# Weights, x and the result laid out by features: an adaptive-layer block on one core without its TensorE turns outside attention and the gates

## The reference

```python
c = einsum('bti,oi->bto', x, W1) + b1 + 2.0 * (x @ lora_As[id1]) @ lora_Bs[id1]        # (b, t, 1024)
# attention inside a sequence, rotary, causal: 32 query heads, 8 key/value heads of 128
a = softmax(mask(rope(c @ wq) . rope(c @ wk) * 128**-0.5)) . (c @ wv)
x1 = x + a @ wo
# two more layers behind each other, each a base weight and gated low-rank parts
d = x1 @ W2.T + 2.0 * sum_e gate_e * (x1 @ A2_e.T) @ B2_e.T               # 8 experts, top 2, language bias
y = x1 + d @ Wf.T + bf + 0.5 * sum_e combine_e * (d @ Af.T) @ Bf_e.T      # 16 experts, top 2 of softmax(d @ Rf.T)
```

## Time and profile before

| | us |
|---|---|
| median of 3 runs | 2720.73 |
| lowest, highest | 2719.8, 2721.68 |
| the profiled execution | 2716.21 |
| its span in the profile | 2714.4 |
| TensorE busy (PE) | 2662.1 |
| VectorE, ScalarE, GpSimd busy | 1341.2, 842.3, 1060.9 |

### The profile page before, as it was taken

One profiled execution on the slowest core, in us unless ns is written; L12 is line 12 of the kernel. 1 busy time (PEld: TensorE's weight loads), 2 busy tenths in 40 slices (PEclk: granted clock), 3 DMA queues, 4 the chain that ended last, 5 costly groups with the idle time before them and its releaser, 6 DMA issues.

```text
span 2714.4 us, 36233 instructions
## 1 busy us (share of the span) xinstructions
PE 2662.1 (98%) x13880; PEld 2135.4 (79%) x13880; DVE 1341.2 (49%) x2035; ACT 842.3 (31%) x2041; POOL 1060.9 (39%) x686
## 2 busy tenths in 40 slices
PE   8989999999999999999999999999999999999999
PEld 7867777777776788887877777777777678888877
DVE  3134677777777111124533577777777511113442
ACT  2132344444444211221212334444444422121110
POOL 0035666666665334520304553344343453341120
PEclk9999999999999999999999999999999999999999
DMA  6953233333335333111534323333332551311322
GB/s 213 235 188 117 90 127 113 111 121 125 125 117 202 132 109 116 47 39 54 145 122 112 123 95 113 113 113 113 113 112 87 182 181 53 116 47 40 96 81 65
DMA packets 335917, 312.45 MB, mean 115 GB/s; under 512 B 71674, under 2 KB 282746, under 8 KB 335746
## 3 DMA queue, kind: packets, MB, share of 16 engines
q1 hardware_dynamic: 274146, 254.55, 30.1%
q10 hardware_dynamic: 61600, 55.58, 6.2%
HBM read 220.75 MB, written 89.33 MB: 114 GB/s over the span
## 4 chain that ended last, share of the span: by engine, by line
PE 88%; POOL 5%; DMA 2%; DVE 1%; issue 1%; SPq 1%; ACT 1%; POOLq 0%; ACTq 0%; DVEq 0%
PE prod L704 27%; PE prod L705 26%; PE prod L706 26%; PE turned L951 3%; PE turned L905 2%; POOL o_lo L1567 1%; PE turned L698 1%; PE prod L1131 1%; POOL w_lo L1484 1%; PE turned L920 1%; POOL s_lo L1520 1%; DMA raw<-in_wo 1%; PE prod L815 1%; POOL x_sum L1502 1%; PE turned L935 0%
## 5 line engine op out<-in xcount | busy, mean ns | idle before, releaser
L1484 POOL TENSOR_TENSOR w_lo<-raw,w_hi 128x1024 fp32r<-128x1024 f32 x96 | 238.9, 2490 | 811.5 <-ACT w_hi L1191 811.5
L704 PE MATMUL prod<-o_hi,w_hi 128*128 128x512 f32 x1024 | 403.1, 394 | 14.2 <-POOL o_lo L1567 10.3
L705 PE MATMUL prod<-o_lo,w_hi 128*128 128x512 f32 x1024 | 399.3, 390 | 0.0
L706 PE MATMUL prod<-o_hi,w_lo 128*128 128x512 f32 x1024 | 399.1, 390 | 0.0
L1860 DVE TENSOR_TENSOR x<-prod,x 128x512 f32<-128x512 f32 x128 | 88.5, 691 | 563.9 <-PE prod L706 563.9
L1520 POOL TENSOR_TENSOR s_lo<-w_sum,s_hi 128x512 fp32r<-128x512 f32 x192 | 249.7, 1307 | 295.1 <-ACT s_hi L1251 295.1
L1191 ACT CAST w_hi<-raw 128x1024 fp32r<-128x1024 f32 x130 | 136.2, 1048 | 609.5 <-PE prod L706 432.1
L704 PE MATMUL prod<-t_hi,s_hi 128*128 128x512 f32 x768 | 311.7, 406 | 8.0 <-POOL s_lo L1520 8.0
L705 PE MATMUL prod<-t_lo,s_hi 128*128 128x512 f32 x768 | 301.3, 392 | 0.0
L706 PE MATMUL prod<-t_hi,s_lo 128*128 128x512 f32 x768 | 300.6, 391 | 0.0
L1520 POOL TENSOR_TENSOR s_lo<-raw_pair,s_hi 128x512 fp32r<-128x512 f32 x144 | 198.2, 1383 | 149.2 <-ACT s_hi L1251 145.3
(11 more groups left out here) (167 smaller groups left out, 4824.7 us busy)
## 6 DMA issues: line engine op xcount, KB each, us to landing
o_scratch<-o_out ACTq DMA_DIRECT2D x64, 512.0 KB, 3.2
raw<-in_wo SPq DMA_DIRECT2D x64, 512.0 KB, 3.8
o_raw<-o_scratch SPq DMA_DIRECT2D x64, 512.0 KB, 7.1
raw<-t_scratch SPq DMA_DIRECT2D x50, 512.0 KB, 3.7
raw_pair<-in_wq SPq DMA_DIRECT2D x48, 512.0 KB, 3.9
w_sums_scratch<-w_sum SPq DMA_DIRECT2D x96, 256.0 KB, 4.4
w_sum<-w_sums_scratch SPq DMA_DIRECT2D x96, 256.0 KB, 4.5
t_scratch<-x ACTq DMA_DIRECT2D x17, 512.0 KB, 5.2
```

What stands on the lines that cost most here:

```text
L704: pe.matmul(dst, wh, xh, start=start, stop=False)
L705: pe.matmul(dst, wh, xl, start=False, stop=False)
L706: return pe.matmul(dst, wl, xh, start=False, stop=stop)
L1484: pool.tensor_tensor(WL[i % 2][:], RAW[i % 2][:], WH[i % 2][:].bitcast(F32), ALU.subtract).then_inc(w_lo, 1)
```

## The change

The host lays x, Wf, Af with Rf, Wr2, W1, A2, Bf and B2 out with the input feature on the partition axis, and takes the result by features. The kernel loses all turns but those of attention and of the gates.

- Wf is loaded in 16 pieces of 256 KB, first the eight of t = 0, then W2's second block, then the eight of t = 1. ScalarE casts from SBUF piece by piece, VectorE splits, and the first product of the fold waits chunk by chunk. The turns, copies, stores and loads of `tw` go; each tile is read from the input where it is needed. B2 comes in one transfer instead of eight.
- The first tile of W1 is loaded in the fold's last iteration, cast after the product of i = 7, and split by GpSimd. `fold_buf` exchanges the two `raw` buffers for this. Tile 1 is loaded there too, but is cast after the fold.
- x of t = 0 is loaded, cast and split inside the fold (hf 0) or in the output stage (hf 1), in place in the room of `xt_lo`. x of t = 1 is loaded by 8 transfers of 256 KB that stand on SyncE's queue behind `b_rows` and ahead of W1's tile 2; ScalarE casts its first four chunks after tile 2 and the rest after tile 3; VectorE splits four of them ahead of `h_mask(0)` and four behind it.
- GpSimd's sum, its store and its DRAM copy go; X1 is loaded from x.
- `out_t` is stored straight after VectorE's addition, and its buffer is written again when the store has landed; `turn_out` and `out_s` go.

```diff
...
-        XR = [sb(f"x_raw{i}", [P, D], offset=o * KB) for i, o in enumerate((0, 4, 8, 12, 36, 40, 44, 32))]
...
+        XTR = [sb(f"xt_raw{t}", [P, KC * NT], offset=o * KB) for t, o in enumerate((48, 128))]
...
+            sp.dma_start(ES[:], arf).then_inc(small_in, 16)
+
+            def load_wf(t, k):
+                a = k * D + t * NT
+                sp.dma_start(X1[:, a:a + NT], Wf[:, a:a + NT]).then_inc(wf_in[t][k], 16)
 
             def load_w2(i):
-                sp.dma_start(view(RAW[i % 2][:], KC), W2.rearrange("(k p) n -> p k n", p=P)[:, :, i * P:(i + 1) * P]
-                             ).then_inc(fold_in[i % 2], 16)
-
-            for b in range(KC // 2):
-                load_wf(b)
+                sp.dma_start(view(RAW[fold_buf(i)][:], KC),
+                             W2.rearrange("(k p) n -> p k n", p=P)[:, :, i * P:(i + 1) * P]
+                             ).then_inc(fold_in[fold_buf(i)], 16)
+
             load_w2(0)
-            for b in range(KC // 2, KC):
-                load_wf(b)
+            for k in range(KC):
+                load_wf(0, k)
             load_w2(1)
+            for k in range(KC):
+                load_wf(1, k)
...
-            def load_tw(n):
-
-                if n < 4:
-                    sp.wait_ge(fold_turned, n + 2)
-                else:
-                    sp.wait_ge(tw_turned, n - 4 + 1)
-                if n < TW_A2:
-                    src, dst = W1[n * P:(n + 1) * P, :], TW_IN[n % 4]
-                elif n == TW_A2:
-                    src, dst = A2, TW_IN[n % 4]
-                else:
-                    o = n - TW_B
-                    src = Bf[:, o * P:(o + 1) * P, :].rearrange("e p r -> p e r")
-                    dst = TW_IN[n % 4].rearrange("p (e r) -> p e r", e=EF)
-                sp.dma_start(dst, src).then_inc(tw_in[n % 4], 16)
-
             def adapter(hf, n):
                 return sp.value_load(ID1[0:1, hf * (BATCH // HALVES) + n:hf * (BATCH // HALVES) + n + 1],
                                      min_val=0, max_val=SLOTS - 1)
@@ -461,21 +435,22 @@
                     sp.dma_start(view(AWS[hf][:, t * D:(t + 1) * D], KC, n8 * RANK1, (n8 + 1) * RANK1),
                                  A1[bass.ds(m * D, D), :].rearrange("(k p) r -> p k r", p=P)).then_inc(a_in, 16)
 
-            def load_x(hf, b):
-                if hf == 0 and b >= 4:
-
-                    r = (b - 3) % 4
-                    sp.wait_ge(m_out[r], 16 * (KC // 4 + (r == 0)))
-                sp.dma_start(XR[b][:], x[hf * TOK + b * P:hf * TOK + (b + 1) * P, :]).then_inc(x_in[b], 16)
-
-            for n in range(4):
-                load_tw(n)
-            for i in range(2, KC + 1):
-                if 4 <= i < 8:
-                    load_x(0, i - 4)
-                if i >= 5:
-
-                    sp.wait_ge(const_in, 16 * 5)
+            def load_x(hf, t):
+                for k in range(KC):
+                    a = k * NT
+                    sp.dma_start(XTR[t][:, a:a + NT], x[hf * KC + k][:, t * NT:(t + 1) * NT]
+                                 ).then_inc(x_in[t][k], 16)
...
+                    load_tile(0, i - KC - 1, tw[TW_W + W1_ORDER[i - KC - 1][0]])
...
-            def store_xt(hf, b):
-                sp.wait_ge(x_sum, hf * TB + b + 1)
-                sp.dma_start(xt_d.rearrange("k p n -> p k n")[:, :, b * P:(b + 1) * P], view(XS[b % 2][:], KC)
-                             ).then_inc(xt_out[b % 2], 16)
...
-                    sp.dma_start(X1[:, j * TOK:(j + 1) * TOK], xt_d[j]).then_inc(x1_in[j], 16)
+                    sp.dma_start(X1[:, j * TOK:(j + 1) * TOK], x[hf * KC + j]).then_inc(x1_in[j], 16)
...
+                if hf:
+                    sp.wait_ge(prod, q_base)
+                load_x(hf, 1)
...
-            def turn_wf(b):
-                pe.wait_ge(wf_in[b], 16)
-                if b >= 1:
-                    pe.wait_ge(fold_split, b)
-                turn_block((b + 1) % 2, X1[:, b * D:(b + 1) * D], P, fold_turned)
...
-                        if i == 0 and t == 0 and k % 2 == 1:
-                            turn_wf(KC // 2 + k // 2)
-                        if i >= 1 and k == KC // 2:
-                            turn_tw(2 * (i - 1) + t)
-                        if i == KC and t == 1 and k == KC - 2:
-                            turn_tw(TW_N - 1)
-
-                    main(3 * i + 1 + t, i % 2, flat(XH, t), parts(XLP, t), chunk=chunk).then_inc(fold_prod, 1)
-
-            pe.wait_ge(tw_copied, TW_N)
+                        if i == 0:
+                            pe.wait_ge(fold_split, t * KC + k + 1)
+
+                    main(3 * i + 1 + t, fold_buf(i), flat(XH, t), parts(XLP, t), chunk=chunk).then_inc(fold_prod, 1)
+
...
-                def first_chunk(k):
-                    if k % 2 == 1:
-                        turn_x(hf, 4 + k // 2)
-
-                pe.wait_ge(xt_lo, hf * TB + 4)
+                pe.wait_ge(xt_lo, xt_no(hf, 0, KC - 1))
                 hold(pe)
-                c_main(0, chunk=first_chunk)
+                c_main(0)
...
-                def turn_out(q):
-                    for t in range(TT):
-                        pe.wait_ge(taken, q_base + (q - 2 + t + 1 + 4))
-                        for b in range(BPT):
-                            mm = pe.transpose(PJ[(q + t) % 4][:, b * P:(b + 1) * P],
-                                              OT[t][:, b * P:(b + 1) * P], ident)
-                        mm.then_inc(prod, 1)
-
...
+            def wf_hi(t, k):
+                act.wait_ge(wf_in[t][k], 16)
+                a = k * D + t * NT
+                act.copy(XH[:, a:a + NT], X1[:, a:a + NT]).then_inc(fold_hi, 1)
...
+            def x_hi(hf, t, k):
+                act.wait_ge(x_in[t][k], 16 * (hf + 1))
+                xs = slice(k * NT, (k + 1) * NT)
+                act.copy(XTH[t][:, xs], XTR[t][:, xs]).then_inc(xt_hi, 1)
...
+                if i == KC:
+
+                    act.wait_ge(fold_prod, 3 * KC)
+                    tile_hi(0, 0)
...
+                    for k in range(4 * n, 4 * n + 4):
+                        x_hi(hf, 1, k)
...
-                    pool.tensor_tensor(view(XS[b % 2][:], KC), view(XTH[t][:].bitcast(F32), KC, c, c + P),
-                                       view(XTL[t][:].bitcast(F32), KC, c, c + P), ALU.add).then_inc(x_sum, 1)
...
+            def wf_lo(t, k):
+                dve.wait_ge(fold_hi, 2 + t * (KC + 1) + k)
+                a = k * D + t * NT
+                dve.tensor_tensor(chunk_of(XLP, k, t), X1[:, a:a + NT], XH[:, a:a + NT].bitcast(F32), ALU.subtract
+                                  ).then_inc(fold_split, 1)
...
+            def x_lo(hf, t, k):
+                dve.wait_ge(xt_hi, xt_no(hf, t, k))
+                xs = slice(k * NT, (k + 1) * NT)
+                dve.tensor_tensor(XTL[t][:, xs], XTR[t][:, xs], XTH[t][:, xs].bitcast(F32), ALU.subtract
+                                  ).then_inc(xt_lo, 1)
...
+                for k in range(KC // 2):
+                    x_lo(hf, 1, k)
                 h_mask(0)
+                for k in range(KC // 2, KC):
+                    x_lo(hf, 1, k)
...
-                def take_out(s):
-                    q = Q_O + 4 * s + 2
-                    for t in range(TT):
-                        is_prod(q + t)
-                        dve.wait_ge(out_done[t], (hf * KC + s) * 16 + 16)
-                        dve.tensor_copy(OS[t][:], PJ[(q + t) % 4][:]).then_inc(taken, 1)
...
-        "x": np.asarray(x).reshape(BATCH * SEQ, D),
+        "x": np.asarray(x).reshape(HALVES, TOK, KC, P).transpose(0, 2, 3, 1).reshape(HALVES * KC, P, TOK),
...
```

More of the change, by code:

```diff
@@ L192, in build @@
         OT = [sb(f"out_t{t}", [P, NT], offset=(184 + 2 * t) * KB) for t in range(TT)]
-        OS = [sb(f"out_s{t}", [P, NT], offset=(188 + 2 * t) * KB) for t in range(TT)]
         BC = [sb(f"c2_cols{i}", [P, P], offset=(196 + i) * KB) for i in range(2)]
@@ L329, in hold @@
             eng.sem_inc(held[eng.engine], 1)
-        def tw_round(n):
-            return 16 * (n // 4 + 1)
-        def tw_all_stored(eng, last=TW_N - 1):
-            for n in range(last - 3, last + 1):
-                eng.wait_ge(tw_stored[n % 4], tw_round(n))
         def m_all_out(eng):
@@ L693, in _ @@
             pe.wait_ge(ident_in, 16)
-            def turn_block(par, raw, rows, done):
-                for c in range(KC):
-                    mm = pe.transpose(TP[par][:, c * P:c * P + rows], raw[0:rows, c * P:(c + 1) * P],
-                                      ident[0:rows, 0:rows])
-                mm.then_inc(done, 1)
             def three(dst, wh, wl, xh, xl, start, stop):
```

273 lines of the change are left out of this document (88 added, 185 removed).

## The result

The changed kernel takes **2677.03 us** (median of 4 runs, 2675.31 to 2679.09) against 2720.94 us before (4 runs). The ratio is 0.9836, with a 95% interval of 0.9823 to 0.9849. The gain is 43.9 us by the medians; I had forecast 50.3 and a time of 2670.4, with a range of 2661 to 2681. The profiled execution took 2678.42 us with a span of 2676.6. That of before (2716.21) was 4.7 us under its median, this one is 1.4 over its own, so the two traces differ by only 37.8 us in span. I compare places inside the traces first, then the medians.

A forecast was written before the change was run, and what follows sets the result against it. TensorE, busy 2662.1 of 2714.4 us, was taken to set the time, so work off its list counts in full. The terms sum to -50.3 us, span 2664.1, forecast 2670.4 us by the median, range 2661 to 2681 (80%).

The forecast's parts named there:

- A: Start, up to the fold's i = 1: without turns the data decide, 23.5 instead of 35.72 us, -12.2 us.
- B: Rest of the fold: two turns go per i, the pitch falls from 14.51 to 12.69 us, -16.9 us.
- C: Fold's end to `c_main(2)`: turns go but `c_lora(0)` newly waits for `h_masked`, 35.15 to 26.1 us, -9.0 us.
- D: Output stage: `turn_out` goes, a column takes 12.67 instead of 13.57 us; -9.0 us in half 0, -6.3 in half 1.
- E: Change of halves, to half 1's `c_main(2)`: a new wait as in half 0, 25.96 to 30.5 us, +4.5 us.
- F: Last instructions: the final store can start when `out_t` is done, not `out_s`, -1.4 us.
- The price of a turn: In the fold: six matmuls with one turn take 2.26 us, without it 1.36, so a turn costs TensorE 0.90 us.
- Small transfers pay alone: Loads of Wf and x: each 256 KB transfer takes 4.5 us, one after another; 77 us slower, 2798; chance 2%.
- The fold stays paced by its loads: Fold, i = 5 to 8: SyncE's list keeps the pitch at 14.51 us; 7.3 us less gain, 2678; chance 10%.
- The two waits are hidden: Waits at `h_masked` in both halves don't show: C gives 16.6, E -6; 18 us more gain, 2652; chance 6%.
- The turns' time isn't given back: Anywhere but the start, TensorE waits for splits or banks instead; some 12 us of gain, 2709; chance 2%.

The follow-up runs named there:

- e4: Changed kernel with eight unused transposes put back between the fold's products, two blocks per i from i = 1 on, 16 in all; 2690.95 us, ratio 0.9892.
- e5: Changed kernel with Wf loaded by 8 transfers of 512 KB instead of 16 of 256 KB; 2674.61 us, ratio 0.9832.
- e6: Changed kernel with GpSimd's low part of W1's tile 2 held until the first four splits of x's t = 1 are done; 2667.57 us, ratio 0.9805.
- e7: Changed kernel with 44 (half 1: 34) unused matmuls between `h_lora(0)` and the wait for `h_masked`; 2669.53 us, ratio 0.9817.
- e10: Changed kernel with half 1's x of t = 0 cast and split one output-stage column sooner (3 to 6, not 4 to 7); 2676.46 us, ratio 0.9835.
- e1: Changed kernel with VectorE making `h_masked` before the eight splits of x's t = 1, not between the fourth and fifth; 2657.38 us, ratio 0.9766.
- e2: Changed kernel with SyncE issuing W1's tiles 2 and 3 ahead of x's t = 1; 2655.04 us, ratio 0.9758.
- e9: Changed kernel with ScalarE casting x's first four t = 1 chunks ahead of W1's tile 2, the next four ahead of tile 3; 2658.39 us, ratio 0.9775.

## Why the prediction was right, and where it was off

The direction, the size and the range were right; the forecast was 6.6 us too low. One of the signs I had named was not met: `c_lora` was to wait 5 to 7 us in half 0, and it waits 10.9 (half 1: 7 to 10, measured 8.1). The terms, in the two traces:

| term | forecast | traces | |
|---|---|---|---|
| A, start | -12.2 | -12.6 | 35.72 to 23.14 |
| B, rest of the fold | -16.9 | -16.9 | 118.45 to 101.59 |
| C, to `c_main(2)` | -9.0 | -3.9 | 35.15 to 31.25 |
| D, output, half 0 and 1 | -15.3 | about -14.9 | 0.87 a column, and turns of x |
| E, change of halves | +4.5 | +8.6 | 25.96 to 34.53 |
| F, last instructions | -1.4 | about -1.8 | |

**A, B, D and F** held to within 0.4 us each. The price of a turn, read as a difference between two chunks with and without one and not as the busy time of its group, is what carried them; e4 confirms it. The reading of the DMA slices put i = 1 at 23.5, and it came at 23.14. That A is this close is in part luck, as the first wait alone varies by 1.9 us between the traces (e5).

**C and E were mis-sized**, by 5.1 and 4.1 us. The wait, its place and its cause were as forecast, but of the terms in it one was wrong: "VectorE splits the last of them (0.69) and makes `h_masked` (0.69)", 4.9 us from tile 2's cast to the mask. It is 8.58 in both halves (144.49 to 153.07, 1422.86 to 1431.44): 3.7 us more, twice. In e6, with GpSimd held back, it is 4.69 (144.99 to 149.68). I had priced the last split at the mean of its group and taken the other three as hidden behind ScalarE's casts. GpSimd's subtractions for tiles 2 and 3 (2.35 and 2.68 us), whose like I had priced at 2.49 on its own for tile 1 in the same paragraph, ran beside the four splits and blocked them: they take 6.4 us together and 2.5 without GpSimd (e6). The rest of C is tile 2, cast at +19.8 instead of +18.3: two tiles were issued together behind x, at 6.9 us median to landing, and not alone at my 4.2. The two make up the 5.1, and in E 3.7 + 0.3 the 4.1. The 0.3 is luck: `b_rows` ended 1.5 us sooner than I said (+11.5, not +13.0), and from there tile 2 took 11.5 us instead of 9.7. The 1.5 us for the clock before `c_main(2)` was right in both (1.4); behind it another 0.6 and 1.3 us are lost up to `c_main(3)`, which I had not counted, 2.0 and 2.7 in all by e7. In E, `c_main(0)` started at +4.4 instead of +2.1, by the same blocking of the two last splits; e10 shows that this cost nothing as long as the later wait stood.

The terms in the traces add up to -41.5, and the spans differ by 37.8. Of the 3.7 between them 1.9 are the clock behind `c_main(2)`; the rest lies in places that the change doesn't touch, the waits at wo among them (2.6 and 1.3 us before, 1.6 and 2.5 now), and was not tried. From `c_main(3)` of half 1 to the end the two traces differ by only 3.9 us, where half 1's share of D and F make 7.9; against the eleven other traces it is 7.0 to 9.0, so the terms hold, and the changed kernel's traced execution lost 3 to 5 us there that the others didn't. By the medians the gain is 43.9; the traced execution of before was 4.7 us faster than its median, and where these lie no trace shows. In the traces the sum missed by 12.5 us, by the medians by 6.6: the mis-sized C and E alone would have put the time at 2679.6, still inside the range, and that the median came closer is luck.

**The rivals.** *Small transfers pay alone*: refuted by the slices above and by e5. *The fold stays paced by its loads*: refuted by the pitch of 12.69. *The two waits are hidden*: not so as the kernel stands. I wrote that I saw no way round the order of the lists; e1, e2 and e9 are three ways round, of a few lines each. *The turns' time isn't given back*: refuted by e4. The Trainium skill's rule on batching ("DMA: Bandwidth & Descriptors", section "Bandwidth"), which I had weighed against the change and not followed, would have put it some 10 us slower, an estimate with the same page's price of about 2.0 us per transfer. That price stands in its section "Anatomy of one DMA — SWDGE (gpsimd) path" and is for transfers issued by GpSimd, while these are issued by SyncE. The runs show the loads at 306 to 394 GB/s with 256 KB a piece, and no gain from twice the size.
